# Two-layer graph kernel on one core: the first layer's mask words turned on VectorE instead of TensorE, its degree taken as a 257th matmul column, and the nodes numbered in another order

## The reference, cut to what matters

```python
h = relu(layernorm(x))
mask = adj > 0;  deg = mask.sum(axis=1)
agg = mask @ h / max(deg, 1)
x = x + relu(concat(h @ W_self + b_self, agg @ W_nb + b_nb) @ W_comb + b_comb)
h = relu(layernorm(x))
# graph attention, 4 heads of 64: Wh = h @ W, scores leaky_relu(sl[n] + sr[m]),
# softmax over the m with adj[n, m] + (n == m) > 0, out = alpha @ Wh
x = x + elu(out)
```

## Time and profile before

| what | value |
|---|---|
| median of 3 runs (lowest to highest) | 874.06 us (872.64 to 874.10) |
| the profiled execution's own time | 866.93 us |
| its span | 865.3 us |
| PE busy | 818.5 us, 95% |
| PEld busy (weight loads, beside PE) | 755.1 us, 87% |
| DVE busy | 713.8 us, 82% |
| ACT busy | 684.9 us, 79% |
| POOL busy | 160.3 us, 19% |

### The profile page before, as it was taken

The page is one execution under the profiler, slowest core; times in us unless marked ns, Lnnn a source line. Parts: engine busy times, 40 slices in busy tenths (PEclk is TensorE's granted clock), DMA queues, the critical chain, the costliest instruction groups (busy, mean ns, idle before and its releaser), DMA issues.

```text
span 865.3 us, 28719 instructions
## 1 busy us (share of the span) xinstructions
PE 818.5 (95%) x11300; PEld 755.1 (87%) x11300; DVE 713.8 (82%) x1371; ACT 684.9 (79%) x966; POOL 160.3 (19%) x221
## 2 busy tenths in 40 slices
PE   5998899999999999769999999999999999999996
PEld 4445799999999999659999999999999999999996
DVE  5997777787777776487897999888999889998885
ACT  3776666666666766488999998999989999989993
POOL 0112546464555555200000000000000000000000
PEclk9999999999999999879999999999999999999998
DMA  7446888878787889340041011301101410111001
GB/s 224 142 149 236 288 308 284 315 281 313 283 306 297 299 306 246 77 108 27 0 97 48 0 49 49 69 29 49 49 2 46 97 49 7 42 48 49 4 20 37
DMA packets 74908, 115.34 MB, mean 133 GB/s; under 512 B 55584, under 2 KB 57504, under 8 KB 66688
## 3 DMA queue, kind: packets, MB, share of 16 engines
q1 hardware_dynamic: 67504, 94.19, 33.3%
q0 software_dynamic: 7376, 20.85, 7.9%
HBM read 98.17 MB, written 16.85 MB: 133 GB/s over the span
## 4 chain that ended last, share of the span: by engine, by line
PE 58%; DVE 19%; ACT 9%; DMA 8%; issue 5%; SPq 0%; DVEq 0%; ACTq 0%
PE ps_a L581 19%; PE ps_x L646 8%; PE ps_a L646 8%; PE ps_t L646 8%; DMA stage<-in_adj 7%; ACT stage L794 5%; DVE stage L1087 4%; PE ps_w L646 4%; PE ps_h L646 4%; DVE stage L1077 2%; PE ps_t L566 2%; DVE mT L1098 2%; PE ps_w L602 2%; DVE g L1113 2%; DVE bits L981 2%
## 5 line engine op out<-in xcount | busy, mean ns | idle before, releaser
L581 PE MATMUL ps_a<-g,mT 128*128 128x256 f16 x2048 | 236.2, 274 | 2.5 <-DVE mT L992 2.5
L581 PEld LDWEIGHTS ps_a<-g,mT 128*128 128x128 fp8e4 x2048 | 201.5, 98 | 26.9 <-issue 2.6
L794 ACT ACTIVATE stage<-rows,sr 128x1024 int8<-128x1024 f32 x192 | 204.1, 1170 | 5.7 <-PE ps_w L646 5.7
L794 ACT ACTIVATE stage<-bits,sr 128x1024 int8<-128x1024 f32 x192 | 204.1, 1166 | 2.5 <-PE ps_w L646 2.4
L734 ACT ACTIVATE junk<-bits 128x2048 uint8<-128x2048 uint8 x64 | 122.2, 1910 | 71.0 <-DVE bits L981 66.3
L1087 DVE SCALAR_TENSOR_TENSOR stage<-stage,mask 128x1024 int32<-128x1024 int32 x128 | 156.1, 1220 | 21.4 <-ACT stage L794 21.0
L1098 DVE TENSOR_SCALAR mT<-stage 128x1024 int32<-128x1024 int32 x128 | 87.9, 687 | 18.4 <-PE ps_w L646 18.0
L981 DVE TENSOR_SCALAR bits<-stage 128x2048 uint8<-128x2048 int32 x64 | 77.4, 1232 | 13.9 <-DMA stage<-in_adj 13.6
L646 PE MATMUL ps_x<-g,stage 128*128 128x130 f16 x1024 | 79.5, 220 | 5.8 <-DVE g L1132 3.6
L646 PE MATMUL ps_x<-g,mT 128*128 128x130 f16 x1024 | 78.7, 219 | 4.8 <-DVE mT L1098 4.8
L646 PE MATMUL ps_a<-g,stage 128*128 128x130 f16 x1024 | 79.6, 220 | 0.0
(11 more groups left out here) (143 smaller groups left out, 1278.1 us busy)
## 6 DMA issues: line engine op xcount, KB each, us to landing
stage<-in_adj SPq DMA_DIRECT2D x64, 1024.0 KB, 6.6
mask<-in_x SPq DMA_DIRECT2D x16, 256.0 KB, 2.8
own_scratch<-mask POOLq DMA_DIRECT2D x16, 256.0 KB, 3.1
rows<-in_x POOLq DMA_DIRECT2D x32, 128.0 KB, 3.2
rows<-own_scratch POOLq DMA_DIRECT2D x32, 128.0 KB, 5.5
x_scratch<-late POOLq DMA_DIRECT2D x32, 128.0 KB, 2.2
bits<-s_scratch SPq DMA_DIRECT2D x8, 512.0 KB, 4.2
rows<-s_scratch SPq DMA_DIRECT2D x8, 512.0 KB, 5.5
```

Of the source, the lines that this page charges most:

```text
L581: last = nc.tensor.matmul(ps_a[e][:, 0:D], m[:, kk, b, :], g[:, 2 * kk + b, part * D:(part + 1) * D], start=(kk == 0 and b + part == 0), s ...
L794: nc.scalar.activation(sign_bytes(sgn, k, b), srow[gr % 2], ACT.Sign, bias=sr[:, 2 * k + b, H + gr // NS:H + gr // NS + 1]).then_inc(act_s ...
```

## The change

- **Order of nodes.** Node `1024*a + 64*k + 2*i + e` now sits at partition `32*a + i`, block k, parity e. Each load or store that touched 128 partitions by node becomes four DMAs of 32 partitions (x tiles, rows of x, output stores). The x tiles 0 and 1 are loaded by ACT's queue.
- **Units.** `adj` comes in 64 units of 1 MB: 64 targets by all 4096 sources, four DMAs of 32 partitions each, in pieces of 4 KB, into three buffers (`stage`, `stage2`) instead of two. The first three are loaded ahead of x tiles 2 to 15.
- **`to_bits`** writes a 32-bit word of two targets by two sources: 2048 bytes out, in pairs with a step of 4 bytes.
- **`turn`**, one DVE 32x32 transpose of 512 words of 32 bits a unit, writes straight into `mask32`. The words' matmuls, `copy_words`, POOL's `keep` and ACT's `degrees` are gone.
- **`sums`**: 32 matmuls of 257 columns (low half of `g` and a column of ones) and 32 of 256 (high half) into one bank; weights have a step of 4 bytes, in the second layer too. Of tile 0 they begin as `g` fills. `turn_h1` stands after 11 of the 16 blocks.
- **`post`** takes the degree from PSUM column 256, and a `to_bits` stands in it where it waited for ACT's root. The order on DVE is `post(t)` with `to_bits(2t+6)` in it, `turn(2t+6)`, `to_bits(2t+7)`, `low_h1T(t)`, `turn(2t+7)`, self edges. PE, DVE and SP are unrolled over the tiles; ACT and POOL keep loops.
- The scores' row is made by two transposes and a strided copy; the last group's stores are shared by SP and ACT.

```diff
-STORES = 32
+UN = 4
+UP = P // UN
+STORES = 32 * UN
+GD = 2 * D + 2
+TURN = 11
-    adj_v = adj.rearrange("(k p e) m -> k p (e m)", p=P, e=2)
+    adj_v = adj.rearrange("(f k j e) (a c) -> k f a j e c", f=UN, j=UP, e=2, a=UN)
+        g = sb("g", [P, NT, GD], F16)
+        stage2 = sb("stage2", [P, HALF], I32)
+        halves = [stage[:, 0, :], stage[:, 1, :], stage2[:, :]]
...
+            def adj_rows(n):
+                if n >= 3:
+                    sp.wait_ge(bits_ready, n - 2)
+                for a in range(UN):
+                    sp.dma_start(halves[n % 3][a * UP:(a + 1) * UP, :].rearrange("p (e c) -> p e c", e=2),
+                                 adj_v[n // UN, n % UN, a]).then_inc(stage_in[n % 3], 16)
+            for n in range(3):
+                adj_rows(n)
             with sp.Fori(0, NP2 - 1) as i:
                 for b in range(2):
                     sp.wait_ge(h_ready, i * 2 + b + 1)
+                    for a in range(UN):
+                        sp.dma_start(xin[a * UP:(a + 1) * UP, b, :],
+                                     x_v[a, bass.ds(i * 2 + (b + 2), 1)].rearrange("o i d -> (o i) d")
+                                     ).then_inc(x_in[b], 16)
+            for n in range(3, 2 * NT):
+                adj_rows(n)
...
-            def words(t, e):
...
+            def sums(t, e, first, end):
+                if first == 0:
+                    pe.wait_ge(turned, (t // 2 + 1) * UN)
+                    if t >= 2:
+                        pe.wait_ge(x1_ready, t - 1)
+                    hold(pe, waits_passed)
+                for kk in range(first, end):
+                    if t == 0:
+                        pe.wait_ge(mm_free, 2 * kk + 6)
                     for b in range(2):
+                        at = bytes_of(mask32[:, kk, t // 2 * P:(t // 2 + 1) * P], e, b)
+                        nc.tensor.matmul(ps_t32[e][:, 0:D + 1], at, g[:, 2 * kk + b, D:2 * D + 1],
+                                         start=kk + b == 0, stop=kk == NK - 1 and b == 1, skip_group_check=True)
+                        last = nc.tensor.matmul(ps_t32[e][:, 0:D], at, g[:, 2 * kk + b, 0:D], start=False,
+                                                stop=kk == NK - 1 and b == 1, skip_group_check=True)
...
+            for t in range(NT):
+                sums(t, t % 2, 0, TURN)
+                if t:
+                    turn_h1(t - 1, 1 - t % 2)
+                sums(t, t % 2, TURN, NK)
+                if t:
+                    wh_product(t - 1, 1 - t % 2)
...
+            def to_bits(n):
+                dve.wait_ge(stage_in[n % 3], (n // 3 + 1) * 16 * UN)
+                if n >= 2:
+                    dve.wait_ge(turned, n - 1)
+                nc.vector.tensor_scalar(bits[:, n % 2, :].rearrange("p (m e s) -> p e m s", e=2, s=2),
+                                        halves[n % 3].rearrange("p (e m s) -> p e m s", e=2, s=2),
+                                        0.0, float(ONE), ALU.is_gt, ALU.mult).then_inc(bits_ready, 1)
+            def turn(n):
+                dve.wait_ge(bits_ready, n + 1)
+                nc.vector.transpose(mask32[:, :, n * UP:(n + 1) * UP],
+                                    bits[:, n % 2, :].bitcast(I32).rearrange("p (k i) -> p k i", k=NK)).then_inc(turned, 1)
...
-                link(nc.vector.tensor_reduce(deg[:, 0:1], degp[:, bass.ds(t, 1), :], AX_X, ALU.add), 1)
-                link(nc.vector.tensor_scalar(deg[:, 1:2], deg[:, 0:1], float(ONE), -GSCALE / ONE, ALU.max, ALU.mult), 2)
-                link(nc.vector.reciprocal(deg[:, 2:3], deg[:, 1:2]), 3)
                 dve.wait_ge(agg_ready, t + 1)
+                link(nc.vector.tensor_scalar(deg[:, 0:1], ps_t32[e][:, D:D + 1], -1.0, GSCALE, ALU.min, ALU.mult), 1)
+                link(nc.vector.reciprocal(deg[:, 1:2], deg[:, 0:1]), 2)
...
                 nc.vector.bn_aggr(mv1[:, :], stats1[:, :]).then_inc(var1_ready, 1)
+                between()
                 dve.wait_ge(std1_ready, t + 1)
...
+            to_bits(0)
+            turn(0)
+            two_pairs(NP2 - 2)
             low_hT(NK - 1, 1)
+            for n in range(1, UN):
+                to_bits(n)
+                turn(n)
             outputs(NK - 2, 0, NP2 - 1)
             outputs(NK - 1, 1, NP2 - 1)
+            for n in range(UN, UN + 2):
+                to_bits(n)
+                turn(n)
+            for t in range(NT - 2):
+                n = 2 * t + UN + 2
+                more = n < 2 * NT
+                post(t, lambda: to_bits(n) if more else None)
+                if more:
+                    turn(n)
+                    to_bits(n + 1)
+                low_h1T(t, t % 2)
+                if more:
+                    turn(n + 1)
+                if t % 2 == 0 and t:
+                    set_self_edges(t // 2 - 1)
...
+def bytes_of(words, e, b):
+    return words.bitcast(F8).rearrange("p (n e b) -> p e b n", e=2, b=2)[:, e, b, :]
```

More of the change, by code:

```diff
@@ L467, in _ @@
             row(0, 1)
-            keep(0, 0)
-            keep(0, 1)
             store_x1(0, 0)
@@ L484, in _ @@
             store_wh(NT - 4, 0)
-            keep(NK - 1, 1)
             store_x1(NK - 1, 0)
@@ L605, in wh_product @@
                 last.then_inc(wh_mm_ready, 1)
-            def tile(t, e, first=False, final=False):
-                sums(t, e, 0)
-                if not final:
-                    words(t + 1, 1 - e)
-                if not first:
-                    turn_h1(t - 1, 1 - e)
-                sums(t, e, 1)
-                if not first:
-                    wh_product(t - 1, 1 - e)
-            pe.wait_ge(consts, 6)
-            words(0, 0)
-            pe.wait_ge(mm_free, 2 * NK + 4)
-            tile(0, 0, first=True)
-            tile(1, 1)
-            with pe.Fori(1, NK - 1) as k:
-                for e in range(2):
-                    tile(k * 2 + e, e)
-            tile(NT - 2, 0)
-            tile(NT - 1, 1, final=True)
+            for t in range(NT):
[5 more added lines that the diff above has]
+                    wh_product(t - 1, 1 - t % 2)
             turn_h1(NT - 1, 1)
@@ L635, in _ @@
             pe.wait_ge(s_compact, 1)
-            nc.tensor.transpose(ps_s, s_c.rearrange("p h t -> p (h t)"), ident[:, :]).then_inc(sT_ready, 1)
+            for e in range(2):
+                last = nc.tensor.transpose(ps_s[:, e * P:(e + 1) * P],
+                                           s_c.rearrange("p h (k e) -> p e (h k)", e=2)[:, e, :], ident[:, :])
+            last.then_inc(sT_ready, 1)
             pe.wait_ge(s_row_ready, 1)
-            def bytes_of(t):
-                return t.bitcast(F8).rearrange("p (n b) -> p b n", b=2)
             def branch(q, j, br, ring, size):
@@ L679, in _ @@
         def _(act):
+            for b in range(2):
+                for a in range(UN):
+                    act.dma_start(xin[a * UP:(a + 1) * UP, b, :], x_v[a, b]).then_inc(x_in[b], 16)
             act.wait_ge(consts, 4)
@@ L727, in _ @@
             highs(NK - 1, 1)
-            def degrees(t):
-                for f in range(2):
-                    if not isinstance(t, int) or t or f:
-                        act.wait_ge(deg_ready, t * 2 + f)
-                    act.wait_ge(bits_ready, t * 2 + (f + 1))
-                    nc.scalar.activation(junk[:, :], bits[:, f, :], ACT.Copy,
-                                         accum_out=degp[:, bass.ds(t, 1), f:f + 1].rearrange("p o f -> p (o f)")
-                                         ).then_inc(deg_ready, 1)
             def norm1(t, e):
@@ L875, in _ @@
             last_exps(1)
+            for i in range(2):
+                act.wait_ge(y_ready, NG + i)
+                for a in range(UN // 2, UN):
+                    last_rows(act, i, a)
         @block.vector
@@ L1182, in _ @@
             signs(0, 1)
-            post(NT - 1, 1, NK - 1)
+            post(NT - 1, lambda: None)
             z_of(0, 0)
```

216 lines of the change are left out of this document (63 added, 153 removed).

## The result

The changed kernel takes **927.71 us** (median of 4 runs, 926.83 to 933.31) against 874.08 for the kernel before (4 runs, 872.64 to 875.39): ratio 1.063, 95% interval 1.058 to 1.067. It is slower; 842 was forecast. The profiled execution took 926.83 us with a span of 925.3; the one before had 865.3.

The account below looks back on a forecast made before the run. TensorE was taken to bound both layers. Words gone, with start and end terms, gained 33.7 us by the first layer's end; less 1.9 in the tail, 31.8: 874.06 to 842 us, range 833 to 866.

Parts of the forecast that it names:

- the DMA term: First-layer loads: bytes stay, 332 GB/s needed, 4 KB pieces add 0.1 us a MB, 7.5 of 7.9 us a tile.
- rival A: First layer: DMA supply or a slow turn sets the period, at worst 8.79 us; total 850 to 865; chance 0.26.
- DMA share above 0.9: First layer: a DMA share above 0.9 was named as one sign that the forecast was right.
- Words off TensorE, 7.9 us a tile: First layer: 0.90 us of words gone in each of 32 tiles, period 8.79 to 7.9 us.
- DVE: First layer: two copies of 0.685 us become two turns of 0.69; busy about 7.0 of 7.9 us a tile.
- rival B: `to_bits` on DVE falls to one element a cycle, 2.28 us instead of 1.23; total 886; chance 0.10.
- Weights with a step of 4 bytes: Second layer, 8192 matmuls: no cost taken; other end a load fully exposed, +40 ns each.
- C: Second layer: wider-step weight loads show through, slower from 3.9 ns each, 1174 if exposed fully; chance 0.04.
- POOL: First layer: five row DMAs a tile at up to 1.28 us, 7.5 us at worst inside 7.9; rows two tiles ahead.
- Start, 1.0 us for a late x in a range of 0 to 3: Prologue: x behind ACT's queue and 3 MB of `adj` ahead of tile 2; first sums at 79.9 against 77.31.
- End of the first layer, 2.1 us in a range of 0 to 6: Last tiles: last load makes DVE 3.9 us late, TensorE has 1.8 in hand; end at 333.9.
- Second layer and tail: Six more stores a group covered; SP issues eight in the tail, so the last goes out 1.9 us later.

Follow-up runs that it names:

- three kernels with fast loads: Changed kernel, each adj unit loaded by one 128-partition DMA (8 KB or 4 KB pieces) or four DMAs of every fourth partition: 852.12, 852.40, 852.13 us.
- step-4 kernel: Changed kernel with its quarter loads of adj written to every fourth partition instead of 32 neighbours: 852.13 us.

## Why the prediction was wrong

**The step that failed** is the DMA term: "By that slope 4 KB pieces add 0.1 us a MB: 7.5 of 7.9 us. It fits, narrowly". It priced a transfer by bytes and length of pieces alone. For loads over all 128 partitions it was right, the length of pieces too: a share of 0.95 to 0.98 is 7.5 to 7.7 of 7.9 us. But the quarters' destination was taken as free: into 32 neighbours a tile's bytes take 10.4 us, not 7.5. The same error stood in rival A, which was the right mechanism with a false floor, "the worst is no faster than now, 8.79". Nothing held the rate at 298 GB/s once the shape of the loads changed; A's worst should have been bounded by a row with a narrower DMA, and where no row had one, left open above 8.79. Then the range would have reached past 870, and a slower kernel would have had more than 0.15. "DMA share above 0.9" was named as a sign that I was right: it was 1.04, at 253 GB/s instead of 332. A share alone doesn't tell work from slowness; GB/s beside it does.

There was a rule for this that I did not weigh. The Trainium skill (SBUF — State Buffer, "Door 1: The DMA port swizzle") states that DMA writes go through 16 ports of eight partitions, that a partition 32 further lies on the same port and one 64 further on the other port of its pair, so that partitions 0 to 31 and 0 to 63 reach the same eight ports. By its 435 GB/s for all, eight give 218, an estimate; from the trace, also as an estimate, `adj` alone had 2.10 of 2.62 MB, 202 of the 253 GB/s. The runs agree on 32 against 64 neighbours and on step 4. Counting the ports reached does not give the rest: 112 and 96 partitions reach all 16, and so do two halves on two queues taken together, and all three stayed at 250 to 273 GB/s. The rule that I did weigh, one transfer of 128 partitions instead of parts, holds here for neighbours only: parts with a step of 4 took 852.1 us, as one DMA did.

Term by term:

- **Words off TensorE, 7.9 us a tile: right.** In each of the three kernels with fast loads TensorE is busy for 40.00 us from 140 to 180, with 366 matmuls.
- **DVE: right.** The turn is 704 ns (0.69 taken), `to_bits` 1232 ns (1.23): rival B is out. At full pace DVE is busy 31.05 of 40 us, 6.1 a tile; 7.0 was allowed.
- **Weights with a step of 4 bytes: right.** 97 ns and 531 matmuls in 30 us; C is out.
- **POOL: right on issues, wrong on the first row.** Issues of rows took 0.5 to 0.7 us, not 1.28. "Uncovered they would hold `post`" was left at nothing; `post(0)` waited 13.1 us, 6.8 with fast loads.
- **Start, 1.0 us for a late x in a range of 0 to 3: wrong.** With fast loads the first sums come at 87.3, 7.4 behind my 79.9. x whole and tile 0 first gives 3.6 of it back. What remains begins with x tile 2, 2.8 us later than before, for which DVE waited 2.39 us, and goes on with a spell at a lower granted clock; that the 3 MB of `adj` ahead of tile 2 hold it back is likely but was not tested there. The cover that I named, "DVE was busy elsewhere until x was needed", is false for tile 0: nothing runs before it.
- **End of the first layer, 2.1 us in a range of 0 to 6: nothing came of it.** In the step-4 kernel the h1 transposes of the last tiles start at 331.90, 339.83 and 347.75, the full pace of 7.9 us.
- **Second layer and tail: right.** After the last sums 500.4 us against 499.6; the last stores take 3.61 us on SP against 1.91.

So with the destination mended, 852.1 us lies in my range of 833 to 866. By the spans, 850.6 against 833.5, it is 17.1 over: 7.4 at the start, 9.1 in the layer, 0.7 behind it. Against 842 it is only ten, because that figure adds the 7.1 us by which the profiled execution of before ran below the median. In the layer TensorE waited three times for h1, 9.6 us in all, 6.2 of them behind the first own row; the 3.7 us stall of the start, which I had going away, was replaced by a longer one.

**Open.** Why a load is slow when its rows don't run over all partitions in an even step. The trace names neither the engine nor the partition of a packet, so the own-sixteenth account is an inference from which kernels were fast; that quarters on two queues reached about 300 GB/s and halves on two queues 250 to 267 isn't explained by it. Other steps than 1 and 4 weren't tried.

## What to carry to other kernels

Before a layout turns whole tiles into blocks of neighbouring partitions, price the loads at the 243 GB/s for a full share that this kernel showed instead of 359, and check that the stage has that much slack; the same data into every fourth partition moved at 342. Judge a DMA-bound stage by GB/s and share together. And when a term is called covered, name what runs in that moment: at the very start nothing does.

## What the runs showed that I had not expected

- The same bytes, addresses, pieces and number of DMAs moved at 335 GB/s into every fourth partition and at 253 into 32 neighbours.
- 64 neighbours (249 GB/s) were as slow as 32 (254), and 112 + 16 (256 to 266) hardly better.
- Quarters into 32 neighbours from two queues moved 287 to 311 GB/s, halves from two queues 250 to 267, quarters from three queues 248 to 288.
- DMAs whose source has an outermost dimension of 4 kept the share at 0.32, two of them to a unit.
- 32x32 transposes of 512 words on 128 partitions ran at 704 ns, as long as the pass of L1159 over 512 words (692 ns).
